# State-space steps on joint products, experts in one stretch, gated layer with its norm one batch ahead

## The reference, cut to what matters

```python
logits = tokens @ wg                       # 4096 tokens, 8 experts, top 2, capacity 1024 each
disp = disp.at[f1].add(tokens * keep1[:, None]).at[f2].add(tokens * keep2[:, None])
h  = gelu(einsum('ecd,edf->ecf', disp, w_gate), approximate=False)   # 256 -> 1024
eo = einsum('ecf,efd->ecd', h, w_down)                                # 1024 -> 256
out = g1 * keep1 * eo[f1] + g2 * keep2 * eo[f2]
```

```python
x = x + local_attention(...) @ wo
h = shift_token(x)                         # second half of the features one token later
h = (h - h.mean()) / sqrt(h.var() + 1e-5) * lg + lb
a, g = split(h @ w1 + b1)                  # 256 -> 2 * 682
x = x + (a * gelu(g)) @ w2 + b2
```

```python
u = silu(conv(...))                        # 512 features
delta, B, C = split(u @ x_proj_w.T, [64, 80])       # 64 + 16 + 16 columns
delta = softplus(delta @ dt_proj_w.T + dt_proj_b)
state = exp(delta * A) * state + (delta * u) * B    # 16 states, scan over 1024 tokens
y = (state * C).sum() + u * D
```

## Time and profile before

| | |
|---|---|
| time, median of 3 runs | 10649.19 us |
| profiled execution | 10658.04 us, span 10656.2 us |
| mean granted TensorE clock | 0.858 of full |
| PE busy | 8354.1 us (78%) |
| PEld busy | 4572.8 us (43%) |
| DVE busy | 5866.7 us (55%) |
| ACT busy | 4348.3 us (41%) |
| POOL busy | 2286.5 us (21%) |
| DMA | 521.77 MB, mean 49 GB/s |

### The profile page before, as it was taken

How to read it: one execution, slowest core, us unless ns; L and a number is a source line. 1 busy time by engine, 2 the same in 40 slices (tenths; PEclk the granted TensorE clock), 3 DMA queues, 4 the chain that set the end, 5 groups by cost and what they waited for, 6 DMA issues and landing times. The chain is left out here.

```text
span 10656.2 us, 120727 instructions
## 1 busy us (share of the span) xinstructions
PE 8354.1 (78%) x42322; PEld 4572.8 (43%) x42322; DVE 5866.7 (55%) x11337; ACT 4348.3 (41%) x7530; POOL 2286.5 (21%) x2066
## 2 busy tenths in 40 slices
PE   4877584975888889889897888888886999656565
PEld 1222253542333356546643544454343444345454
DVE  6777441015667546426624877775543666555554
ACT  3666230111555545326512665562221444333332
POOL 1110102011011011001100443340000100366666
PEclk8888676986999989989997988899886999788787
DMA  3222232112122100000000000000001322356666
GB/s 65 40 46 34 41 61 91 64 48 42 30 41 40 25 13 2 10 12 2 10 0 13 1 1 1 1 3 8 5 1 24 57 47 43 113 184 188 185 181 187
DMA packets 243502, 521.77 MB, mean 49 GB/s; under 512 B 55051, under 2 KB 94837, under 8 KB 241431
## 3 DMA queue, kind: packets, MB, share of 16 engines
q1 hardware_dynamic: 154887, 232.49, 11.0%
q0 software_dynamic: 88064, 282.15, 8.8%
HBM read 425.31 MB, written 75.53 MB: 47 GB/s over the span
## 5 line engine op out<-in xcount | busy, mean ns | idle before, releaser
L818 ACT ACTIVATE probs<-scores 128x1024 f32<-128x1024 f32 (+4 forms) x960 | 868.4, 937 | 877.4 <-PE scores L695 618.3
L907 DVE TENSOR_REDUCE row_max<-ring 128x1 f32<-128x512 f32 (+3 forms) x1792 | 1025.6, 627 | 244.3 <-PE ring L669 219.1
L695 PE MATMUL scores<-query_stack,key_stack 99*128 99x512 bf16 (+3 forms) x2816 | 847.3, 392 | 164.9 <-DVE levels L929 77.5
L3663 POOL DMA_INDIRECT r_got<-in_L_ffn_tables,r_pick_now x832 | 814.9, 979 | 329.4 <-issue 245.0
L3788 PE MATMUL r_psum_y<-r_diagonal,r_got 128*128 128x128 f32 x4096 | 582.6, 312 | 370.0 <-ACT r_diagonal L3845 370.0
L715 PE MATMUL outputs<-probs,head_values 128*32 128x512 f32 (+3 forms) x5632 | 778.9, 628 | 102.3 <-ACT probs L815 99.8
L3788 PEld LDWEIGHTS r_psum_y<-r_diagonal,r_got 128*128 128x128 f32 x4096 | 566.7, 226 | 430.9 <-ACT r_diagonal L3845 425.1
L815 ACT ACTIVATE probs<-levels,quant 128x1024 f32<-128x1024 uint8 x512 | 612.8, 1234 | 328.5 <-DVE levels L929 325.1
L929 DVE TENSOR_SCALAR levels<-scores 128x1024 uint8<-128x1024 f32 x512 | 607.6, 1220 | 177.5 <-PE scores L695 145.5
L669 PE MATMUL ring<-key_stack,query_stack 96*128 96x512 bf16 (+3 forms) x1792 | 607.9, 382 | 62.5 <-DMA key_stack<-normed_parts 39.8
L3597 DVE TENSOR_TENSOR_SCAN ssm_pre<-ssm_pre,added 128x1024 f32<-128x1024 f32 x256 | 570.9, 2271 | 32.3 <-ACT ssm_pre L3555 32.3
(11 more groups left out here) (653 smaller groups left out, 15562.1 us busy)
## 6 DMA issues: line engine op xcount, KB each, us to landing
joined_heads<-heads_out SPq DMA_DIRECT2D x512, 32.0 KB, 2.0
expert_w<-in_L_ffn_w SPq DMA_DIRECT2D x16, 1024.0 KB, 11.0
r_got<-in_L_ffn_tables,r_pick_now POOLq DMA_INDIRECT x832, 3.7
quant_parts<-parts SPq DMA_DIRECT2D x48, 256.0 KB, 5.4
query_stack<-quant_parts SPq DMA_DIRECT2D x48, 256.0 KB, 8.8
key_stack<-quant_parts SPq DMA_DIRECT2D x48, 256.0 KB, 8.5
query_stack<-cross_parts SPq DMA_DIRECT2D x48, 256.0 KB, 8.3
normed_parts<-parts SPq DMA_DIRECT2D x48, 256.0 KB, 5.6
```

Of the source, the lines that this page charges most:

```text
L695: last = nc.tensor.matmul(out[:, off:GROUP], keys, q_stack[0:rows, h, half * GROUP + off:(half + 1) * GROUP], start=True, stop=not edge)
L818: nc.scalar.activation(dst, s_ps[0:k_rows, 2 * (e % 2):2 * (e % 2) + 2, off:GROUP], ACT.Exp, scale=scale).then_inc(probs_ready, 1)
L907: nc.vector.reduce_max(row_max[:, i, qt, at:at + 1], src[:, 0:cols], AX.X).then_inc(ring_read, 1)
L3663: nc.gpsimd.indirect_dma_start(out=b["got"][:, n, :], out_offset=None, in_=b["tables"], in_offset=bass.IndirectOffsetOnAxis(ap=b[picks][:, ...
```

## The change

Three independent parts.

Experts: the two rounds become one block over eight experts, written out, with two buffers for `taken_t` and `h`. TensorE's order puts the transposes of the next expert and the hidden product of the next half ahead of the output product of this half. The weights of the first two experts are fetched by SP in the block that zeroes the buffer, behind the zeroing stores.

Gated layer: w1 and the vectors are fetched by SP in the block of `window_attention` (new argument `following`); w2 in the first block of `gated_ffn`. The loop over four batches becomes five blocks written out, `b` from -1 to 3: each makes the products of batch `b` and the norm of batch `b + 1`, whose pieces stand at fixed places among the products. Shifted inputs alternate between `chip.z` and `chip.sq`. The adds write into `inner` itself, and the copy at the end goes.

State space: one product by all 96 columns of `x_w` takes the place of two; ACT copies it once; DVE splits 32 rows of it, after all four `shift`s; the B rows come from 8 transposes. The polynomial has three terms by new coefficients (`LOG_SERIES`), two operations instead of four. DVE multiplies dt by u for all chunks.

```diff
+        def fetch_weights(sp, e):
+            sp.dma_start(w1[:, e % 2, :, :], io["L0_ffn_w1"][e * DIM:(e + 1) * DIM, :].rearrange("(c p) f -> p c f", p=P)).then_inc(weights_loaded[e % 2], 16)
+            sp.dma_start(w2[:, e % 2, :, :], io["L0_ffn_w2"][e * EXPERT_INNER:(e + 1) * EXPERT_INNER, :].rearrange("(c p) d -> p c d", p=P)).then_inc(weights_loaded[e % 2], 16)
...
                         sp.dma_start(whole[n], zeros[:, :]).then_inc(zeroed, 16)
+                    fetch_weights(sp, 0)
+                    fetch_weights(sp, 1)
...
-            taken_t = eb("taken_t", [P, FC, CAPACITY])
-            h = eb("expert_hidden", [P, ic, GROUP])
+            taken_t = eb("taken_t", [P, 2, FC, CAPACITY])
+            h = eb("expert_hidden", [P, 2, ic, GROUP])
...
+                    turn(0)
+                    hide(0)
+                    for g, (e, j) in enumerate(groups):
+                        if j == parts - 1 and e + 1 < EXPERTS:
+                            turn(e + 1)
+                        if g + 1 < len(groups):
+                            hide(g + 1)
+                        produce(g)
...
         with nc.Fori(0, DEPTH) as layer:
-            window_attention(chip, layer, inner)
-            gated_ffn(chip, layer, inner)
+            with ExitStack() as gated:
+                weights = [gated.enter_context(sbuf(nc, name, shape, F32)) for name, shape in (
+                    ("gated_w1", [P, FC, 2 * HC * P]), ("gated_b1", [P, 2 * HC]), ("gated_b2", [P, FC]), ("gated_norm", [P, 2 * FC]))]
+                window_attention(chip, layer, inner, gated_sources(chip, layer, weights))
+                gated_ffn(chip, layer, weights, inner)
         with banks(nc, "norm_psum", [P, 8, GROUP], F32) as ps, nc.Fori(0, GROUPS // 2) as pair:
...
+                for dst, src in following:
+                    sp.dma_start(dst, src).then_inc(following_loaded, 16)
+                sp.wait_ge(following_loaded, 16 * len(following))
 
             @block.tensor
             def _(pe):
...
+        for b in range(-1, BATCH):
+            gated_step(chip, weights, w2, w2_source if b < 0 else None, inner, b if b >= 0 else None, b + 1 if b + 1 < BATCH else None, inputs[b % 2], inputs[(b + 1) % 2],
...
+                        last = nc.tensor.matmul(y_ps[:, c, :], w2[:, n, c * P:(c + 1) * P], hidden[:, j, n, :], start=(n == 0), stop=(n == HC - 1))
+                    last.then_inc(y_ready, 1)
+
+            for k in range(len(pairs)):
+                pair(k)
+                if k in (2, 3):
+                    mean(k - 2)
+                if k in (7, 8):
+                    variance(k - 7)
+            output(0, 0)
+            spread(0)
+            output(0, 1)
+            spread(1)
+            output(1, 0)
+            output(1, 1)
...
+            for k, (j, n) in enumerate(pairs):
+                if k in (0, 1):
+                    shift(k)
+                if k in (4, 5):
+                    centre(k - 4)
+                if multiplies:
                     dve.wait_ge(gate_ready, k + 1)
                     nc.vector.scalar_tensor_tensor(out=hidden[:, j, n, :], in0=h_ps[:, 2 * (k % 2), :], scalar=b1[:, n:n + 1], in1=gate[:, k % 2, :],
                                                    op0=ALU.add, op1=ALU.mult).then_inc(hidden_ready, 1)
-                for j in range(HALVES):
-                    for c in range(FC):
-                        dve.wait_ge(y_ready, FC * j + c + 1)
-                        nc.vector.scalar_tensor_tensor(out=after[:, c, bass.ds(at(j), GROUP)], in0=y_ps[:, c, :], scalar=b2[:, c:c + 1],
-                                                       in1=inner[:, c, bass.ds(at(j), GROUP)], op0=ALU.add, op1=ALU.add).then_inc(y_added, 1)
-        with step(nc, "copied") as (block, copied):
-            @block.scalar
-            def _(act):
-                nc.scalar.activation(inner[:, 0, :], after[:, 0, :], ACT.Copy).then_inc(copied, 1)
-
-            @block.vector
-            def _(dve):
-                nc.vector.tensor_copy(inner[:, 1, :], after[:, 1, :]).then_inc(copied, 1)
+            inverse(0)
+            inverse(1)
+            add(0, 0)
+            normalise(0)
+            add(0, 1)
+            normalise(1)
+            add(1, 0)
+            add(1, 1)
...
-        low, rest = sb("ssm_low", [RANK, SEQ]), series[0:rows, :]
+        low, rest = sb("ssm_low", [rows, SEQ]), series[RANK:rows, :]
+        middle = ctx.enter_context(sbuf(nc, "ssm_middle", [rows, SEQ], BF16))[RANK:rows, :]
...
-                shift(0)
-                shift(1)
-
-                dve.wait_ge(rest_ready, 1)
+                for c in range(SC):
+                    shift(c)
+
                 third = lambda t, n: t[n * 2 * STATES:(n + 1) * 2 * STATES, :]
-                then(copy(states[:, :], rest))
-                then(tt(rest, rest, states[:, :], ALU.subtract))
-                then(copy(third(states, 1), third(rest, 1)))
-                then(copy(third(states, 2), third(rest, 2)))
-                then(tt(third(rest, 2), third(rest, 2), third(states, 2), ALU.subtract))
-                copy(third(states, 2), third(rest, 2)).then_inc(states_ready, 1)
-                shift(2)
-                shift(3)
+                whole = low[RANK:rows, :]
+                dve.wait_ge(low_copied, 1)
+                then(copy(third(states, 2), whole))
+                then(tt(rest, whole, third(states, 2), ALU.subtract))
+                then(copy(middle, rest))
+                then(copy(third(states, 1), middle))
+                then(tt(rest, rest, middle, ALU.subtract))
+                copy(third(states, 0), rest).then_inc(states_ready, 1)
+                dve.wait_ge(states_ready, 1)
 
 
                 edge = 2.0 ** -6
                 for c in range(SC):
                     dve.wait_ge(exp_ready, c + 1)
                     e, log = pre[:, c, :], logs[:, c, :]
-                    then(nc.vector.tensor_scalar(series[:, :], e, -1 / 4, 1 / 3, ALU.mult, ALU.add))
-                    then(tt(series[:, :], series[:, :], e, ALU.mult))
-                    then(stt(out=series[:, :], in0=series[:, :], scalar=-0.5, in1=e, op0=ALU.add, op1=ALU.mult))
-                    then(stt(out=series[:, :], in0=series[:, :], scalar=1.0, in1=e, op0=ALU.add, op1=ALU.mult))
+                    then(stt(out=series[:, :], in0=e, scalar=LOG_SERIES[0], in1=e, op0=ALU.add, op1=ALU.mult))
+                    then(stt(out=series[:, :], in0=series[:, :], scalar=LOG_SERIES[1], in1=e, op0=ALU.add, op1=ALU.mult))
                     dve.wait_ge(log_ready, c + 1)
 
-                    then(stt(out=log, in0=e, scalar=edge, in1=log, op0=ALU.is_lt, op1=ALU.subtract))
-                    then(stt(out=series[:, :], in0=log, scalar=-1.0, in1=series[:, :], op0=ALU.mult, op1=ALU.max))
+                    then(stt(out=log, in0=e, scalar=edge, in1=log, op0=ALU.is_lt, op1=ALU.add))
+                    then(stt(out=series[:, :], in0=series[:, :], scalar=1 / LOG_SERIES[1], in1=log, op0=ALU.mult, op1=ALU.min))
                     dve.wait_ge(shifted_ready, c + 1)
                     tt(dt[:, c, :], dt[:, c, :], series[:, :], ALU.add).then_inc(dt_done, 1)
                     dve.wait_ge(dt_done, c + 1)
-                dve.wait_ge(du_ready, SC - 1)
-                tt(pre[:, SC - 1, :], dt[:, SC - 1, :], u[:, SC - 1, :], ALU.mult).then_inc(du_ready, 1)
-
-            @block.gpsimd
-            def _(pool):
-                for c in range(SC - 1):
-                    pool.wait_ge(dt_done, c + 1)
-                    nc.gpsimd.tensor_tensor(pre[:, c, :], dt[:, c, :], u[:, c, :], ALU.mult).then_inc(du_ready, 1)
+                    tt(pre[:, c, :], dt[:, c, :], u[:, c, :], ALU.mult).then_inc(du_ready, 1)
...
-                        nc.tensor.matmul(low_ps[0:RANK, j, :], w_x[:, c, 0:RANK], own, start=(c == 0), stop=(c == SC - 1))
-                        last = nc.tensor.matmul(st_ps[0:rows, j, :], w_states[:, c, :], own, start=(c == 0), stop=(c == SC - 1))
+                        last = nc.tensor.matmul(low_ps[0:rows, j, :], w_x[:, c, :], own, start=(c == 0), stop=(c == SC - 1))
...
                 for t in range(TILES):
-                    for c in range(SC):
-                        last = nc.tensor.matmul(st_ps[:, 0, t * STATES:(t + 1) * STATES], u[:, c, t * P:(t + 1) * P], w_x[:, c, RANK:RANK + STATES],
-                                                start=(c == 0), stop=(c == SC - 1))
+                    last = nc.tensor.transpose(st_ps[:, 0, t * 2 * STATES:(t + 1) * 2 * STATES], low[RANK:rows, t * P:(t + 1) * P], chip.c(C_ID)[RANK:rows, RANK:rows])
```

More of the change, by code:

```diff
@@ L2237 @@
 TOKEN_TILES = TOKENS // P
-ROUND_EXPERTS = 4
 def token_rows(chip, rows, logits=None, gate_w=None):
@@ L2427, in expert_ffn @@
             per, parts = GROUP // P, CAPACITY // GROUP
[L2428 to L2433, removed]
+            with step(nc, "taken_loaded_0 taken_loaded_1 turned turned_copied h_ready hidden_ready y_ready made_ready stored_0 stored_1") as (
```

(41 more changed lines are left out.)

223 lines of the change are left out of this document (114 added, 109 removed).

## The result

The changed kernel takes 10448.61 us (median of 4 runs, 10433.92 to 10483.1), the kernel before, run beside it on the same chip, 10646.07 us (median of 4, 10630.14 to 10654.5). The ratio is 0.9824, 95% interval 0.9805 to 0.9843: 187 us less, between 167 and 208 (the two medians differ by 197). Forecast were 10492 and a range from 10462: the direction was right, the gain was larger than any case that the range allowed for. Run again on another chip, where the kernel before takes 10878.07 us, the ratio was 0.9823 (0.9804 to 0.9841). All ratios are of fast executions; two executions far above the others (13367 us of the experts alone, 12063 us of the gated layer alone) are left out of them.

What follows compares the result with a forecast made beforehand. TensorE is busy 78% of the span, but each stage was read by its last-ending wait. Gains of 19.3 (experts), 67.1 (gated layer) and 70.4 (steps), 156.8 us, took 10658.0 to 10501.2, as a median 10492; range 10462 to 10530.

Steps and rivals of the forecast that it cites:

- experts, gained on TensorE: Experts: idle time before output products, the round boundary, slow matmuls and a weight wait go, 35.3 us gained.
- experts, lost at SP: Zeroing step: SP blocks issuing weight loads behind the zeroing stores, 16 us lost, between bounds of 2 and 20.
- gated layer, two depths: Gated layer: norms beside products and no final copy, 307.9 us per depth against 341.4, 67.1 us gained for two.
- steps, four batches: State-space steps: 17.4 us gained per batch, 69.6 for four, plus 0.8 for setup copies, 70.4 us.
- rival 1: Zeroing step: SP is not blocked by the stores, 2.5 us lost instead of 16, giving 10479; chance 0.27.
- rival 2: State-space steps: VectorE's slow operation is due to its operands, not POOL; 24 us not saved, giving 10516; chance 0.07.
- rival 4: Gated layer: the norm beside products is late, 7 us in each of six steps, 42 us, giving 10534; chance 0.05.
- the 43.2 contain 2.0 us at the low clock: Gated layer: a product step's 96 matmuls take 43.2 us, 2.0 of it at the low clock, against 41.2.
- Rival 3: Gated layer: the clock falls at four statistic blocks and the restart, 2.0 us each fall, 48 us, giving 10540; chance 0.10.
- 8.0 before T: State-space steps, before the dt products start (T): 16 of 32 products of u go, 8.0 us gained per batch.
- 9.4 after T: State-space steps, from the dt products' start (T) to the last multiply by u: 50.1 us against 59.5, 9.4 gained per batch.
- if dt products ran warm, up to 3.7 us more: State-space steps: dt products at the full clock would gain up to 3.7 us more per batch; not in the sum.

Runs made afterwards that it cites:

- the experts alone: The kernel before with only the expert part of the change: ratio 0.9989 (0.9977 to 1.0) to the kernel before.
- the gated layer alone: The kernel before with only the gated layer's part of the change: ratio 0.9936 (0.9916 to 0.9955) to the kernel before.
- the one with doubled products: The changed kernel with each of the 16 products of u issued twice, second result unused: dt products 9.1, 8.3, 11.8, 8.3 us in four batches; no ratio given.

## Why the prediction was wrong

By its own terms, in us of the profiled executions:

| term | forecast | measured |
|---|---|---|
| experts, gained on TensorE | 35.3 | 34.1 |
| experts, lost at SP | 16 | 19.0 |
| gated layer, two depths | 67.1 | 79.2 |
| steps, four batches (forecast with setup, 0.8) | 70.4 | 79.9 |
| sum | 156.8 | 174.2 |

**Mechanisms.** All three parts went as described, and no rival came true. SP was held (rival 1 had 2.5 us for it); VectorE's slow operation was POOL's doing (rival 2); no product step passed 78 us, and none waited for a norm (rival 4).

**The gated term.** The step that failed is "the 43.2 contain 2.0 us at the low clock", put into each of the four product steps. The traces show it in the first step of a depth alone, as 1.8 us (12.33 less 10.54), since the others start 1.5 to 1.7 us behind products and not behind a norm: they take 72.4, 72.4 and 64.0 us (63.8 in the second depth) where 74.4, 74.4 and 65.8 were forecast, 11.8 us in two depths, nearly the whole of the 12.1 by which this term is off. The earlier trace rows showed the low clock only behind a norm; the change takes the norm away from there, and the sum kept its consequence. Rival 3 (2.0 more at each statistic block) had the same fault with a larger sum: the clock was at 1.00 through the blocks. The rule cited from the Trainium skill, "TensorE: Matmul & The Clock Gate", section "A second HAM failure mode: psum-queue depth-cycling", that short gaps let the clock swing, is not what these steps did: with gaps of 1.54 to 1.70 us between them the granted clock was 1.00.

**The steps' term.** "8.0 before T" was 9.2 (the mean from the first Silu to the dt products fell from 20.5 to 11.4 us): it priced the removed half at 0.51 per product, but the remaining ones also fell from 0.51 to 0.43 without the alternation. "9.4 after T" is short by 0.8 to 1.0 us where the dt products run low (49.1 and 49.3 us, where 50.1 was forecast); where they keep the clock it is 45.8. The text had this as "if dt products ran warm, up to 3.7 us more" and left it out of the sum. It happens in most batches, and goes with the joint product (with the alternation put back it does not happen), which the forecast did not see.

**The experts' term.** 34.1 of 35.3, and SP at 19.0 within the bounds 2 and 20: the fourth load was taken to be the one held, it was the third, until the zeros were all but through.

**The rest.** The terms account for 17 of the 43 us between 10492 and 10448.6. The other 26 are no part of the change. The forecast carried over that the profiled execution lies 8.9 us above the median; the changed kernel's lies 34.5 above its own. The range had no term for it: with every term right the forecast would have been 10475, inside the range, and some 26 us of spread below that reach the measured median, 13 below the range's end. The missed range is thus the two terms and this spread together, and neither alone.

## What to carry to other kernels

A cost seen in every copy of a loop belongs to what stands before it; when a change moves that neighbour, price the cost again instead of multiplying it. Time spent issuing transfers is path time wherever a barrier closes the step, so put loads of many small pieces where SP has nothing to hold up, or split them around large stores (12.0 us against 30.3 here), not all behind them (that this shortens the whole was not shown). And give the range a term for the spread of one execution to the next, taken from the runs of before.

## What was not expected of the hardware

Products with 64 and 96 columns of weights in alternation take 1.02 us for two, equal ones 0.86, both at the full granted clock, and after the alternation the clock falls early among the products that follow (0.57 granted over the dt products of the first batch before, 1.00 in most batches after equal ones); why it does so is open:

```profile
5817.49:5829.83 12.34, 12.34 (x17) 4.50 (x17) 7.87 (x9) 3.08 (x3) 0.00 (x0) 0.57 0.00 1
```

```profile
6059.48:6067.75 8.27, 7.37 (x17) 2.83 (x18) 3.85 (x3) 2.59 (x3) 0.00 (x0) 1.00 0.00 0
```

(The first window is of the kernel before, the second of the one with doubled products.) The other surprise is that VectorE and POOL worked in turn and not side by side, in all 24 of the multiplies above. Chips differ: the kernel before takes 10646 us on one and 10868 to 10878 on others. Between the changed kernel's two profiled executions, 218 us apart, 204 of it lie in the retrieval (1485 and 1689 us).
